# A four-layer residual block on one core: fc1 and VectorE in another order, ten more constant products at the start, and every output matrix copied by SyncE's DMA queue

## The reference, cut to what matters

```python
x = x + L0(x)   # tanh scorer, masked softmax over the 32 tokens, pooling
x = x + L1(x)   # attention, 16 heads of 8, sparse or dense by batch row
x = x + L2(x)   # x -> relu(x @ (wi + common + expert_wi[e]).T) @ (wo + common + expert_wo[e]).T
x = x + L3(x)   # h = gelu(x @ fc1.T + b); concat(h @ fc2.T, h @ experts[e3].T) + bias
```

## Time and profile before

| what | value |
|---|---|
| median of 3 runs | 302.75 us (301.97 to 302.86) |
| profiled execution: its time, its span | 303.31 us, 301.5 us |
| mean granted TensorE clock | 0.977 of 2.4 GHz |
| TensorE busy with products | 269.0 us, 89% of the span |
| VectorE, ScalarE, GpSimd busy | 66%, 43%, 39% |
| period of one step of the loop | 30.1 us |

### The profile page before, as it was taken

How to read it: one execution, slowest core, us unless ns; L and a number is a source line. 1 busy time by engine, 2 the same in 40 slices (tenths; PEclk the granted TensorE clock), 3 DMA queues, 4 the chain that set the end, 5 groups by cost and what they waited for, 6 DMA issues and landing times.

```text
span 301.5 us, 12584 instructions
## 1 busy us (share of the span) xinstructions
PE 269.0 (89%) x4861; PEld 198.3 (66%) x4861; DVE 198.2 (66%) x370; ACT 130.7 (43%) x220; POOL 116.6 (39%) x229
## 2 busy tenths in 40 slices
PE   8697999986889988998899889988998899978985
PEld 6384754545667766776677667766776677847854
DVE  3388695578767777777777777777777767473030
ACT  2033433224627452745274527452745265532231
POOL 7050049033542354235423542354235424560420
PEclk9859799999999999999999999999999999999999
DMA  5503970046305530553045304530553451055000
GB/s 174 185 4 135 282 215 2 0 139 227 130 2 174 214 142 4 174 209 139 0 174 209 139 0 176 207 139 0 177 205 139 187 210 60 35 213 192 22 0 37
DMA packets 26749, 38.25 MB, mean 127 GB/s; under 512 B 10577, under 2 KB 10833, under 8 KB 26594
## 3 DMA queue, kind: packets, MB, share of 16 engines
q1 hardware_dynamic: 26722, 37.87, 35.3%
HBM read 10.60 MB, written 2.10 MB: 42 GB/s over the span
## 4 chain that ended last, share of the span: by engine, by line
PE 42%; issue 24%; DVE 10%; POOL 10%; POOLq 10%; ACT 3%; DVEq 0%
PE pB L686 8%; POOLq L328 5%; PE pS L554 5%; POOL sc L310 5%; PE pB L746 4%; POOLq L338 3%; PE pB L719 3%; PE pB L714 3%; PE pB L644 2%; PE pV L630 2%; POOL x3b L318 2%; PE pB L640 2%; POOL rw L329 2%; PE pS L615 2%; PE pA L554 2%
## 5 line engine op out<-in xcount | busy, mean ns | idle before, releaser
L310 POOL TENSOR_TENSOR sc<-sc,rmax 128x512 f32<-128x512 f32 x32 | 33.6, 1050 | 83.6 <-DVE rmax L1024 83.6
L329 POOL COPY rw<-e3t_s 128x128 f32 x128 | 37.4, 293 | 52.2 <-issue 45.2
L439 ACT ACTIVATE ex<-sc 128x512 f32<-128x512 f32 x32 | 20.2, 631 | 44.8 <-POOL sc L310 44.5
L746 PE MATMUL pB<-rw,hT 128*32 128x128 f32 x1024 | 31.8, 274 | 0.4 <-ACT hT L447 0.4
L1030 DVE STREAM_TRANSPOSE pt<-ex 128x512 f32<-128x512 f32 x32 | 22.7, 708 | 14.2 <-ACT ex L439 14.0
L686 PE MATMUL pB<-rwo,hT 128*32 128x128 f32 x1024 | 29.8, 273 | 0.5 <-ACT hT L443 0.5
L1019 DVE SCALAR_TENSOR_TENSOR sc<-pS,bias 128x512 f32<-128x512 f32 x32 | 21.5, 671 | 12.1 <-PE pS L615 12.0
L644 PE MATMUL pB<-x_l,ffn_h 128*128 128x512 f32 x56 | 23.0, 411 | 7.0 <-DVE x_l L1077 5.8
L746 PEld LDWEIGHTS pB<-rw,hT 128*32 128x32 f32 x1024 | 27.3, 110 | 2.8 <-issue 2.2
L339 POOL COPY rwo<-weff 128x512 f32 x32 | 21.6, 680 | 18.6 <-ACT weff L461 9.6
L686 PEld LDWEIGHTS pB<-rwo,hT 128*32 128x32 f32 x1024 | 27.8, 110 | 1.1 <-ACT hT L443 1.1
(11 more groups left out here) (140 smaller groups left out, 522.1 us busy)
## 6 DMA issues: line engine op xcount, KB each, us to landing
rwo<-weff SPq DMA_DIRECT2D x96, 256.0 KB, 2.3
rw<-fc2t_dram SPq DMA_DIRECT2D x4, 768.0 KB, 8.7
xT<-xt_dram SPq DMA_DIRECT2D x8, 256.0 KB, 2.5
xN<-xn_dram SPq DMA_DIRECT2D x8, 256.0 KB, 2.9
out_dram<-o_s SPq DMA_DIRECT2D x8, 256.0 KB, 2.4
e3t_s<-e3t_dram SPq DMA_DIRECT2D x1, 1024.0 KB, 7.0
rwo<-ffn_w_dram SPq DMA_DIRECT2D x1, 896.0 KB, 6.2
rwo<-ffn_w_dram SPq DMA_DIRECT2D x1, 512.0 KB, 11.6
```

What stands on the lines that cost most here:

```text
L310: pool.tensor_tensor(sc[:, g % 2, :, :], sc[:, g % 2, :, :], rmax[:, g % 2, :].unsqueeze(2).to_broadcast([P, H, S]), ALU.subtract).then_in ...
L329: pool.tensor_copy(rw[:, r, :, SHARED:D], e3t_s[:, bass.ds(e, 1), :, :].rearrange("p o c n -> p (o c) n"))\
L746: last = mm(pB2[S * q:S * q + S, P * g:P * g + P], hT[:, c, tok], rw[:, Q4 * g + q, c, :], start=(c == 0), stop=(c == FC - 1))
```

## The change

It does four things. `DMA_ROWS` holds all 16 rows, and GpSimd's `out_weights` with its semaphore goes. `fc1` does the high-by-high and low-by-high products of three chunks first, then waits for the low part of the activation and does the three third products, then the fourth chunk. VectorE does `pool_weights` part 1 behind `normalise` 0 and not ahead of `turn` 0. The first `keep_busy` has 36 products and not 26.

```diff
-DMA_ROWS = [r for r in range(ROWS) if r % Q4 != Q4 - 1]
+DMA_ROWS = [r for r in range(ROWS)]
...
-            def out_weights(i):
-
-                for g in range(G):
-                    at(pool, out_ps, G * (i - 1) + g + 1)
-                    row = Q4 * g + Q4 - 1
-                    e = pool.value_load(e2i[0:1, bass.ds(ROWS * i + row, 1)], min_val=0, max_val=E2 - 1)
-                    pool.tensor_copy(rwo[:, row, :, :].rearrange("p c d -> p (c d)"),
-                                     weff[:, bass.ds(e, 1), :, :].rearrange("p o c d -> p (o c d)")).then_inc(rwp_sb, 1)
...
                     at(pe, rwo_sb[g], 16 * len(DMA_ROWS) // G * (i + 1))
-                    at(pe, rwp_sb, G * i + g + 1)
...
-            def fc1(i, c):
-                if c == 0:
-                    at(pe, x3_sb, 2 * (i + 1))
-                if c == 2:
-
-                    at(pe, sc_sb, G * NBLK if isinstance(i, int) and i == NBLK - 1 else G * (i + 2))
-                parts3(GIN[c][:, :], weight(N_FC1, c), whole(x3p), True, True, (x3l_sb, i + 1)).then_inc(g_ps, 1)
+            def fc1(i):
+
+                at(pe, x3_sb, 2 * (i + 1))
+                for c in range(FC - 1):
+                    if c == 2:
+                        at(pe, sc_sb, G * NBLK if isinstance(i, int) and i == NBLK - 1 else G * (i + 2))
+                    high, low_part = weight(N_FC1, c)
+                    mm(GIN[c][:, :], high, x3p[0][:, :], start=True, stop=False)
+                    mm(GIN[c][:, :], low_part, x3p[0][:, :], start=False, stop=False)
+                at(pe, x3l_sb, i + 1)
+                for c in range(FC - 1):
+                    mm(GIN[c][:, :], weight(N_FC1, c)[0], x3p[1][:, :], start=False, stop=True).then_inc(g_ps, 1)
+                parts3(GIN[FC - 1][:, :], weight(N_FC1, FC - 1), whole(x3p), True, True).then_inc(g_ps, 1)
...
-            keep_busy(26, pS0, x2p[0])
+            keep_busy(36, pS0, x2p[0])
...
-                if next_block:
-                    pool_weights(n + 1, 1)
                 turn(n, 0)
                 score_max(n, 2)
                 turn(n, 1)
                 score_max(n, 3)
                 turn(n, 2)
                 normalise(n, 0)
+                if next_block:
+                    pool_weights(n + 1, 1)
                 turn(n, 3)
```

More of the change, by code:

```diff
@@ L197, in cond_resid_kernel @@
         out_ps, outn_sb, outT_ps = sem("out_ps"), sem("outn_sb"), sem("outT_ps")
-        x3_sb, x3b_sb, rwp_sb = sem("x3_sb"), sem("x3b_sb"), sem("rwp_sb")
+        x3_sb, x3b_sb = sem("x3_sb"), sem("x3b_sb")
         x3l_sb, x3t_ps, x3n_sb = sem("x3l_sb"), sem("x3t_ps"), sem("x3n_sb")
@@ L382, in step_of @@
                 if isinstance(n, int) and n == 1:
-                    pool.wait_ge(weff_sb, E2)
-                out_weights(n - 1)
-                if isinstance(n, int) and n == 1:
                     pool.wait_ge(bias_sb, 3)
@@ L401, in _ @@
                 step_of(n)
-            out_weights(NBLK - 1)
             for part in range(G):
@@ L857, in step_of @@
                 attn_out(n)
-                for c in range(FC):
-                    fc1(n - 1, c)
+                fc1(n - 1)
             step_of(1, None)
@@ L876, in _ @@
             keep_busy(4, pA0, ffn_p[0])
-            for c in range(FC):
-                fc1(NBLK - 1, c)
+            fc1(NBLK - 1)
             token_major(NBLK - 1)
```

## The result

The kernel after the change takes 307.89 us (median of 4 runs, 305.79 to 309.94); the kernel before had 302.36 us in the same comparison. The ratio is 1.0202, its 95% interval 1.0105 to 1.0299: slower by 1 to 3%. The profiled execution took 309.94 us with a span of 308.2 us, the longest of the four; its mean granted clock is 0.965, the others have 0.967, 0.983 and 0.983.

What follows compares the result with a forecast made beforehand. TensorE, 91% busy at full clock from 76 us, was taken to bound the kernel. Start -3.0, step 1 +1.6, loop +3.5, step 7 and tail -1.5, falls +3.9 sum to +4.5 on 302.75: 307.2 us, range 301.9 to 310.6.

Steps and rivals of the forecast that it cites:

- a wait at group 3: In out_rows, TensorE idles about 2.5 us ahead of its last group for the last copy, 3.0 in step 1.
- falls of the clock: Behind the gaps of six steps, none to six falls to 1.2 GHz at +1.3 us; three taken, +3.9.
- The copies and the loop's step: SyncE's 16 issues, 1.30 us apart, land late for out_rows; five loop steps +0.7 us each, +3.5.
- Step 1 and step 2: Late last copy: step 1 +1.6 us; step 2, as each of the five loop steps, +0.7 us.
- Step 7 and tail: Gathers there are hidden; fc1 saves 0.8 us in step 7 and 0.7 behind it: -1.5 us.
- The start: Up to x1T of block 0 and shortly after, ten more constant products keep the clock up: -3.0 us, bounds 0 and -3.9.
- That the clock would not fall: Rival: the wait in out_rows stands but the loop's clock stays up; 303.4 us, 301.7 to 305; chance 0.28.
- That the queue keeps up: Rival: SyncE's copies land before TensorE asks, six steps each 1.9 us shorter; 286.9 us; chance 0.10.
- GpSimd's copies: Taking them from GpSimd costs and gives nothing else, as GpSimd then reaches subtract_max earlier than VectorE.

Runs made afterwards that it cites:

- the copies alone: The kernel before with all 16 rows copied by SyncE's queue and nothing else changed: 311.78 us, ratio 1.0326.
- the filled gap: The whole change with eight constant products ahead of group 3 of out_rows in steps 1 to 6: 305.13 us, ratio 1.0107.
- the start alone: The kernel before with 36 constant products at the start and nothing else: 300.37 us, ratio 0.9962.
- the kernel with four copies earlier: The whole change with a block's first four copies issued ahead of load_xT in SyncE's loop: 293.81 us, ratio 0.9744.
- the last one: The whole change with four copies ahead of load_xT and, for block 0 alone, each group's fourth row copied by GpSimd: 289.71 us, ratio 0.9630.

## Why the prediction was right, and where its terms were off

The forecast was 307.2 us, slower, by a wait at group 3 and falls of the clock; measured were 307.89. The mechanism is the one forecast. That the number is so close is in part luck, as the falls below show.

**The copies and the loop's step.** This was right. In steps 4 to 6 the spacing is (19.87 - 0.49) / 15 = 1.292 us (1.30 taken), a copy lands after 2.3 to 2.4 us, the gap is 2.0 us (2.5 forecast) and the step +0.6 (+0.7 forecast). The gap is smaller since TensorE comes later. `out_rows` starts 207.50 - 188.70 = 18.80 us behind `x1T`'s end, before 20.47: 1.67 gained where 1.86 were forecast. Its first three groups last 2.83 us, not the 2.62 that I took. Neither moves any time while the queue sets the step: the copies alone, the filled gap and the change itself have the same 30.7 us step, with 0.4, 0 and 2.0 us of idle time ahead of group 3.

**Step 1 and step 2.** These were too low. Less what the falls cost, step 1 of the change is +1.7 (+1.6 forecast) and step 2 +1.5 (+0.7 forecast); in the filled gap they are +2.4 and +1.2. In step 2 the issues are 1.35 us apart instead of 1.29 ((20.81 - 0.49) / 15 in the change). In step 1 of the change the last copy is issued at 60.92 + 18.69 = 79.61 and lands at about 82.3, after 2.7 us and not 2.3. Why is open.

**Step 7 and tail.** The forecast was -1.5, and -1.8 was seen.

**The start.** The forecast was -3.0; -3.4 was seen in the profiled execution of the change, -1.3 in the medians of that part alone. One premise failed: the clock did not stay up ahead of 23 us, but fell from 16.8 to 20.2. L944 was held up as supposed: as L934 it now takes 0.18 us where the earlier trace rows has 1.55. But part of the wait for GpSimd, whose L336 runs from 17.83 to 20.67 us, moved to VectorE's L987:

```profile
17.08 0.18 DVE L934 TENSOR_SCALAR ctab<-ntab 128x32 f32<-128x32 f32 x1
...
18.02 1.51 DVE L987 TENSOR_TENSOR l0e<-l0e,l0c 128x128 f32<-128x128 f32 x1
```

The same operation took 0.29 us before, as L997. So `x1T` of block 0 ends 2.05 us earlier (25.94 to 23.89), where 2.6 were forecast. The later stretch at 1.2 GHz is gone in this execution, which gives the rest; L595's 2.07 us are 1.16. In the run with the start alone it stayed.

**The clock.** Three falls were taken and three came in the profiled execution. That was luck: three was a guess between none and six, and two of the four executions, with their higher mean clock, seem to have had fewer. The size was off: 1.3 us each were forecast, 2.4, 2.4 and 1.5 measured. Two of the stretches at 1.2 GHz were 6.8 us long, twice that of the row I went by (3.2). By the prediction the profiled execution would have taken 307.8 us, and it took 309.94; the median comes so near because the others were shorter.

The Trainium skill's page "TensorE: Matmul & The Clock Gate", section "Why this matters for your kernels", warns only of gaps longer than the 2.5 us that I forecast. The gaps of steps 1 and 2, 3.13 and 3.04 us, are of the length that it warns of. That of step 3 is not, and there the trace does not agree: the clock fell behind 2.06 us of idle time. By length alone step 3 can't be told from steps 4 to 6, where it did not fall.

**The rivals.** That the clock would not fall (303.4): the filled gap makes that case, at 305.1. Its profiled span is 1.5 us longer than that of before where this rival had 0.6, and most of the difference is steps 1 and 2. That the queue keeps up: it did not, at 1.29 us from copy to copy. The Trainium skill's page "DMA: Bandwidth & Descriptors", section "Issuing engines are not separate DMA queues", holds issue time to be usually small beside the DMA itself. The trace does not agree: here SyncE's queue is a third of the chain that ended last (SPq 33%) and the DMA 5%.

**GpSimd's copies.** I said that their going gives nothing but L1053's 0.3 us, and L1043, the same operation, takes 0.68 us instead of 0.97. That is also why the two orders bring TensorE 1.67 us earlier in the change and only 1.3 us beside GpSimd's copies. The Trainium skill, page "SBUF — State Buffer", section "Who interferes with whom", says that a VectorE operation with both inputs in SBUF and a GpSimd operation that reads SBUF exclude each other; the two rows agree.

So the reason is right in kind and place, and three terms are off in size: steps 1 and 2 (1.0 too low without falls), the falls (2.4 too low in the profiled execution), and the start, 0.4 more gain in the profile and 1.7 less in the medians of that part alone. Steps 3 to 6 and the end took back 0.8. The profiled span grew by 6.7 us where 4.5 were forecast, the median by 5.5.

## What to carry to other kernels

Count the issues of a DMA queue like instructions of an engine, from the wait that they are queued behind. Four more copies of 256 KB in a step took the DMA queue's share of the 16 engines from 35% to 42% of the span, but cost SyncE's queue 4 x 1.29 = 5.2 us. A queue that sets the step swallows what the other engines gain in it; without the copies the same parts gave 9.7 us. Before moving work onto a queue, look where it stands still; four issues moved ahead of a wait gave back 14 us (307.9 to 293.8). A wait of 2 to 3 us on TensorE can cost 1.5 to 2.4 us more through its clock, and constant products in it are a cheap test of that.

## What was not expected of the hardware

Of gaps of like length some are followed by a fall of the clock and some are not. It fell behind 2.06 us (step 3 of the change) and around a gap of 1.65 us at the start of the run with VectorE's order alone. It did not fall behind 2.04 us, nor behind 2.68 us (step 1 of the copies alone). Between 16.8 and 20.2 us of the change it fell with no gap ahead but that of 0.61 us. A fall may last 3.4 or 6.8 us: it was 6.8 behind 3.13 us, but 3.4 behind 3.75 us in step 1 of the kernel with four copies earlier. No run here was made to tell what decides this.

A copy's landing has a median of 2.3 us in every run. From 126 to 250 us of the change every copy takes 2.3 us, but the copies from 60 to 116 us have a median of 2.7 and reach 3.5, and one behind the loop took 4.4. In most kernels the first pass of SyncE's loop also issues more slowly than the later ones: 20.81, 20.90 and 20.49 us against 19.87 for 16 copies, 15.71 against 14.72 for 12 with four copies earlier, and 14.85 to 15.51 against 14.79 in those with GpSimd's help, though not in the last one (14.68). What causes either is open; no run here was made to tell.
